# Attention stacks through DRAM: query parts written once, repeated by the reads' pattern, the rows below them read separately

## The chip, the cores and the metric

The kernel runs on one core of one Trainium2 chip. The metric is the device time of one execution in microseconds. The core has five engines with queues of their own: TensorE (PE; its weight loads are PEld), VectorE (DVE), ScalarE (ACT), GpSimd (POOL) and SyncE (SP), which issues all DMAs of this kernel. All of SP's transfers go through one queue to 16 DMA engines.

## The reference

Twelve residual sublayers on x of shape (32, 128, 128), each on the layer-normalised x: three kinds of attention, mixtures of experts, a bidirectional Mamba and a quantised network. The change is in five attentions with 16 heads of 8 dimensions. L3a is self-attention with rotated queries and keys, L1x (with a mask), L2x and L3x attend to a context of 77 rows, and L0a is causal linear attention. Cut to one of them:

```python
def _L3_xattn_ref(xq, xkv, Wq, Wkv, Wout, bout):
    scale = HEAD_DIM ** (-0.5)
    q = (xq @ Wq.T).reshape(B, SQ, NUM_HEADS, HEAD_DIM)
    kv = (xkv @ Wkv.T).reshape(B, SKV, 2, NUM_HEADS, HEAD_DIM)
    k, v = (kv[:, :, 0], kv[:, :, 1])
    att = jax.nn.softmax(jnp.einsum('bxhd,byhd->bhxy', q, k) * scale, axis=-1)
    x = jnp.einsum('bhxy,byhd->bxhd', att, v).reshape(B, SQ, H)
    return x @ Wout.T + bout
```

In L0a the scores are elu(q)+1 times elu(k)+1, masked causally, without a softmax.

## The kernel before

**Streams and order.** The 32 sequences are worked in 4 passes of two streams, 4 sequences (512 columns) each. `run_stream` (L2502) yields a due time for every step of a sublayer, and `in_turn` (L2482) merges the two streams' steps by these times. This is done once for each engine when the program is built, so each engine has one fixed order of both streams' instructions, and semaphores alone decide when they run. The second stream follows the first by 430 us of planned time (`LAG`), so its L2x meets the first stream's L0a of the next pass, and the Mamba (L2a) of either stream lies beside attentions of the other.

**Scores from parts.** A head has only 8 dimensions. `class Heads` (L792) splits each projected value into three bf16 parts (high, mid, low; `heads_high_act`, `heads_rest_dve`, `heads_mid_act`, `heads_low_dve`), and a score is the sum over all nine products of a query part with a key part. So the contraction has 3 x 3 x 8 = 72 rows (`USED`), built as a stack: row (i, j, d) of the query stack is query part i, row (i, j, d) of the key stack is key part j. Rows 72 to 127 (`ROWS` = 128) hold constants: a row of ones and zeros in the query stack, the masked keys' row (L1x) and zeros in the key stack. They were filled in DRAM at the start (`fill_first` L2829, `fill_rest` L2839) and are never written again, save the mask's row.

**Through DRAM.** The parts lie in SBUF as 128 partitions (dimension, head) x 3 parts x columns. The stack needs dimensions of one head on 72 partitions. SP does this with DMAs: `heads_write_sp` (L1351) writes the three parts to DRAM three times, once for each copy, 384 KB each for queries (L1357); `heads_read_sp` (L1361) waits for the last of them (L1365) and then reads the stack in 4 groups of 4 heads, all 128 rows, 4 KB a row, 512 KB a group (L1370). In L0a and L3a query and key parts are both written in the sublayer's main part and the 8 reads alternate: query group 0, key group 0, query group 1 and so on. In L1x, L2x and L3x the keys come from the context, and their writes and reads are issued ahead of the query's (`heads_early_sp`, L1374).

**Who uses them.** `stacks(u)` (L956) makes PE wait for a group's query and key landings at every fourth of 16 units. `scores` (L962, matmul L967) makes q k for the maxima, which DVE reduces (L1252), and `shifted` (L979, matmul L988) makes the transposed scores for the exponentials; L0a has only the latter. `scores` runs up to 6 units ahead of `shifted`.

**Mamba beside it.** `mamba_sp` (L2013) reads rows of B from DRAM onto all partitions, a pair of states at a time (L2026, 512 KB), on the same SP queue. POOL multiplies them into a state's input (L1997), DVE scans it (L2114, L2119).

The rest of the diff renames semaphores of the quantised network L3f (`qf_*` to `ff_*` and `proj_p`), so that one more is to be had.

Of the kernel before, what the change touches and what calls it, by code (L numbers as in the profile page):

```python
# [29 lines left out]
NB = 4  # L30
# [145 lines left out]
class Numbers:  # L176
# [43 lines left out]
    qf_pe="PE: quantised network", qf_a="ACT: quantised network", qf_d="DVE: quantised network",  # L220
    qf_p="Pool: quantised network",
# [5 lines left out]
    rb1="an odd pair of rows of B is on all partitions",  # L227
    wq="query parts are in DRAM", wk="key parts are in DRAM", wm="the masked keys' row is in DRAM",
# [720 lines left out]
def heads_pe(pe, g, m, A, free):  # L949
# [6 lines left out]
    def stacks(u):  # L956

        if u % 4 == 0:
            pe.wait_ge(*g.landed("rq%d" % (u // 4), A.key))
            pe.wait_ge(*g.landed("rk%d" % (u // 4), A.key))  # L960
# [477 lines left out]
def turn_pe(pe, g, m, key, src, free):  # L1438

    s = g.s  # L1440
    yield 0.04
    if key == "L3f":
        pe.wait_ge(*g.at("qf_d", "r3"))
    else:
        pe.wait_ge(*g.at("ln_xn", (key + "i" if key in NESTED else key)))
    g.wait_free(pe, free, s, 2)
    for b in range(NB):
        last = pe.transpose(m.bank[s][2][:, b * T:(b + 1) * T], src[s][:, b, :], m.const["ident"])
    last.then_inc(*g.one("ln_tr", key))
    free[s, 2] = ("ln_xT", key)  # L1450
# [781 lines left out]
def quantised_pe(pe, g, m, Q, free):  # L2232
    s = g.s
    for j in range(4):
        k = j % 2
        yield 0.06 + 0.01 * j
        pe.wait_ge(*g.at("ln_xT", "L3f"))
        g.wait_free(pe, free, s, k)
        pe.matmul(m.bank[s][k][:, :], Q.w("w1", 128 * j, 128 * j + 128), m.xT[s][:, :], start=True, stop=True)\
          .then_inc(*g.one("qf_pe", ("h", j)))  # L2240
        free[s, k] = ("qf_a", ("h", j))
    for b in range(NB + 1):
        if b < NB:
            yield Q.time(b, -0.8)
            if b == 0:
                pe.wait_ge(*g.at("qf_a", ("hs", 3)))
# [5 lines left out]
            last.then_inc(*g.one("qf_pe", ("tok", b)))  # L2252
            free[s, b % 2] = ("qf_d", ("q1", b))
        if b >= 1:
            yield Q.time(b - 1, 0.8)
            pe.wait_ge(*g.at("qf_d", ("q3", b - 1)))
# [4 lines left out]
            last.then_inc(*g.one("qf_pe", ("back", b - 1)))  # L2261
            free[s, 2] = ("qf_a", ("qT", b - 1))
    yield 0.98
    g.wait_free(pe, free, s, 3)
    pe.wait_ge(*g.at("qf_a", ("qT", NB - 1)))
# [4 lines left out]
    last.then_inc(*g.one("qf_pe", "out"))  # L2270
# [3 lines left out]
def quantised_act(act, g, m, Q):  # L2274
    s = g.s
    for j in range(4):
        yield 0.06 + 0.01 * j
        act.wait_ge(*g.at("qf_pe", ("h", j)))
        act.activation(Q.hp(s, j)[:, :, 1:T + 1], m.bank[s][j % 2][:, :].rearrange("p (b t) -> p b t", t=T),
                       ACT.Copy).then_inc(*g.one("qf_a", ("h", j)))  # L2280
    for j in range(4):
        yield 0.16 + 0.06 * j
        act.wait_ge(*g.at("qf_d", ("conv", j, 2)))
        act.activation(Q.hs(s, j), Q.hs(s, j), ACT.Silu, bias=Q.w("convb", j, j + 1))\
           .then_inc(*g.one("qf_a", ("hs", j)))
    for b in range(NB):
        yield Q.time(b, 0.85)
        act.wait_ge(*g.at("qf_pe", ("back", b)))
        act.activation(Q.qT(s)[:, :, b * T:(b + 1) * T],
                       m.bank[s][2][:, :].bitcast(BF16)[:, 0:512].rearrange("p (j t) -> p j t", t=T),  # L2290
                       ACT.Copy).then_inc(*g.one("qf_a", ("qT", b)))


def quantised_pool(pool, g, m, Q):
# [5 lines left out]
    last.then_inc(*g.one("qf_p", "pad"))  # L2300


def quantise_tokens_dve(dve, g, m, Q):
# [3 lines left out]
    def step(name, last):  # L2307
        last.then_inc(*g.one("qf_d", name))

    def after(name):  # L2310
        dve.wait_ge(*g.at("qf_d", name))
# [35 lines left out]
def quantised_dve(dve, g, m, Q):  # L2347
    s = g.s
    for j in range(4):
        for tap in range(3):  # L2350
            yield 0.12 + 0.06 * j + 0.01 * tap
            src, w = Q.hp(s, j)[:, :, tap:tap + T], Q.w("conv", 3 * j + tap, 3 * j + tap + 1)
            if tap == 0:
                dve.wait_ge(*g.at("qf_a", ("h", j)))
                dve.wait_ge(*g.at("qf_p", "pad"))
                ins = dve.tensor_scalar(Q.hs(s, j), src, w, None, ALU.mult)
            else:
                dve.wait_ge(*g.at("qf_d", ("conv", j, tap - 1)))
                ins = dve.scalar_tensor_tensor(out=Q.hs(s, j), in0=src, scalar=w, in1=Q.hs(s, j),
                                               op0=ALU.mult, op1=ALU.add)  # L2360
            ins.then_inc(*g.one("qf_d", ("conv", j, tap)))
    for b in range(NB):
        def step(name, last):
            last.then_inc(*g.one("qf_d", (name, b)))

        def after(name):
            dve.wait_ge(*g.at("qf_d", (name, b)))

        yield Q.time(b, 0.0)
        dve.wait_ge(*g.at("qf_pe", ("tok", b)))  # L2370
# [24 lines left out]
        if b >= 2:  # L2395
            dve.wait_ge(*g.at("qf_pe", ("back", b - 2)))
        step("q3", dve.tensor_scalar(Q.qb(s, b), Q.qa(s, b), ROUND, None, ALU.subtract))
    yield 0.96
    dve.reciprocal(Q.sm(s, 8), Q.sm(s, 7)).then_inc(*g.one("qf_d", "inv2"))
    dve.wait_ge(*g.at("qf_d", "inv2"))  # L2400

    dve.tensor_scalar(Q.sm(s, 8), Q.sm(s, 8), m.wsc[:, 3:4], None, ALU.mult).then_inc(*g.one("qf_d", "f"))
    yield 0.99
    dve.wait_ge(*g.at("qf_d", "f"))
    dve.wait_ge(*g.at("qf_pe", "out"))
# [493 lines left out]
```

## Time and profile before

| | |
|---|---|
| three runs, median (lowest to highest) | 4764.98 us (4752.53 to 4768.23) |
| profiled execution, its own time | 4766.72 us |
| its span, first to last instruction | 4764.2 us |
| granted TensorE clock, mean | 0.833 of full speed |
| PE, DVE busy | 3496.6 us (73%), 2955.6 us (62%) |
| ACT, POOL busy | 1970.0 us (41%), 1234.1 us (26%) |
| DMA queue of SP | 174572 packets, 323.59 MB, 20.1% of 16 engines |

Busy times are unions of the engine's instructions. The DMA share is the mean over 16 engines: 1.00 in a short window means that all 16 move data all the time, and values slightly over 1 come from packets cut at the window's edge. In a timeline each row is a run of like instructions with its start, its length and, in brackets, the idle time of the engine before it and what ended that wait. "issue" there means that the profile shows nothing that was waited for, which also happens when the record of a released instruction is missing.

### The profile page before, as it was taken

The page shows a single profiled execution, that of the slowest core. Times are in us where ns is not written, and L with a number is a line of the kernel's source. Part 1 is how long each engine was busy: PE and PEld are TensorE (multiplying, and loading weights), DVE is VectorE, ACT ScalarE, POOL GpSimd, SP SyncE. Part 2 cuts the span into 40 slices and gives each one's busy share as a digit, 9 for nine tenths or more (in the row PEclk, how much of TensorE's full clock was granted, in tenths as well). Part 3 has the DMA queues.
Part 4 walks back from the last instruction along what each step waited for, and adds up shares of the span by engine and source line. Part 5 has one row for each costly group of instructions (what it writes and reads, how often), then busy time and mean ns, then how long its engine had stood idle before and what let it go on. Part 6 is the DMA issues. An engine that isn't in the chain of part 4 may idle for free. (4 is left out here: it accounts for less than half of the span.)

```text
span 4764.2 us, 69288 instructions
## 1 busy us (share of the span) xinstructions
PE 3496.6 (73%) x25546; PEld 2337.3 (49%) x25546; DVE 2955.6 (62%) x6919; ACT 1970.0 (41%) x3470; POOL 1234.1 (26%) x1568
## 2 busy tenths in 40 slices
PE   5868867666878878665886887856589698685674
PEld 3645635334665555433575654533357465352353
DVE  4436874884554785577545488477654548738646
ACT  2423545343343444543344355434235335443333
POOL 0001451550000243253000045145100005516410
PEclk7989978777988988777898998877789799786776
DMA  7110121313121021032122112122211200211321
GB/s 237 46 47 14 39 81 42 103 55 106 66 79 62 28 76 58 29 130 73 47 100 69 39 36 81 45 88 84 104 56 52 98 10 28 80 54 45 117 101 49
DMA packets 174905, 328.00 MB, mean 69 GB/s; under 512 B 13260, under 2 KB 114988, under 8 KB 173740
## 3 DMA queue, kind: packets, MB, share of 16 engines
q1 hardware_dynamic: 174572, 323.59, 20.1%
q8 instruction: 206, 3.38, 0.3%
q14 instruction: 127, 1.04, 0.1%
HBM read 231.87 MB, written 91.67 MB: 68 GB/s over the span
## 5 line engine op out<-in xcount | busy, mean ns | idle before, releaser
L1881 PE MATMUL bank<-sb_big,sb_weights_const 128*128 128x512 f32 x512 | 376.6, 826 | 333.9 <-DVE sb_big L2119 333.2
L1434 POOL TENSOR_TENSOR sb_rs<-sb_ve,sb_weights_const 128x4 f32<-128x4 f32 x112 | 113.4, 1012 | 1757.6 <-DVE sb_ve L1420 1757.3
L1997 POOL TENSOR_TENSOR sb_big<-sb_big 128x512 f32<-128x512 f32 x384 | 496.4, 1307 | 244.9 <-DVE sb_big L2097 244.3
L1958 ACT ACTIVATE bank<-sb_big,sb_Aneg 128x512 f32<-128x512 f32 x512 | 351.7, 689 | 497.4 <-DVE sb_big L2114 392.3
L1252 DVE TENSOR_REDUCE sb_small<-bank 128x4 f32<-128x308 f32 (+1 forms) x512 | 265.9, 523 | 344.5 <-PE bank L967 340.9
L2114 DVE TENSOR_TENSOR_SCAN sb_big<-bank,sb_big 128x512 f32<-128x512 f32 x384 | 464.6, 1210 | 6.6 <-ACT bank L1958 6.3
L988 PE MATMUL bank<-sb_big 128*77 128x128 bf16 (+1 forms) x2560 | 358.1, 234 | 83.7 <-DMA sb_big<-key_parts 30.3
L988 PEld LDWEIGHTS bank<-sb_big 128*77 128x77 bf16 (+1 forms) x2560 | 274.2, 117 | 140.2 <-issue 89.8
L967 PE MATMUL bank<-sb_big 128*128 128x77 bf16 (+1 forms) x2048 | 187.4, 227 | 179.5 <-DMA sb_big<-query_parts 114.2
L1677 PEld LDWEIGHTS bank<-sb_weights_L1f,sb_big 128*128 128x128 f32 x2048 | 257.3, 191 | 109.0 <-issue 104.9
L1137 ACT ACTIVATE sb_big<-bank 77x512 f32<-77x512 f32 (+1 forms) x352 | 207.9, 593 | 228.3 <-PE bank L1009 152.4
L991 PE MATMUL bank<-sb_topT,sb_pick 128*77 128x128 bf16 (+1 forms) x2048 | 300.0, 227 | 0.0
L1881 PEld LDWEIGHTS bank<-sb_big,sb_weights_const 128*128 128x128 f32 x512 | 97.0, 236 | 407.7 <-DVE sb_big L2119 402.0
L967 PEld LDWEIGHTS bank<-sb_big 128*128 128x128 bf16 x2048 | 145.5, 112 | 304.2 <-issue 146.5
L1677 PE MATMUL bank<-sb_weights_L1f,sb_big 128*128 128x128 f32 x2048 | 275.2, 277 | 21.6 <-DVE sb_x L1746 21.6
L1746 DVE SCALAR_TENSOR_TENSOR sb_x<-bank,sb_small,sb_x 128x128 f32<-128x128 f32 x512 | 143.9, 343 | 229.8 <-PE bank L1677 226.0
L2119 DVE TENSOR_TENSOR sb_big<-bank,sb_big 128x512 f32<-128x512 f32 x384 | 263.5, 686 | 30.9 <-PE bank L1870 8.9
L1341 POOL TENSOR_TENSOR sb_topp<-sb_small,sb_weights_const 128x16 bf16<-128x16 f32 x128 | 29.5, 231 | 971.4 <-DVE sb_small L1252 971.3
L1666 PE MATMUL bank<-sb_xT,sb_weights_L1f 128*128 128x512 f32 x512 | 268.0, 610 | 3.8 <-ACT sb_big L1706 3.8
L1706 ACT ACTIVATE sb_big<-bank,sb_weights_L1f 128x512 f32<-128x512 f32 x256 | 172.3, 686 | 202.7 <-PE bank L1666 202.2
L1666 PE MATMUL bank<-sb_xT,sb_weights_L0f 128*128 128x512 f32 x512 | 242.0, 598 | 7.4 <-ACT sb_big L1700 7.4
L991 PEld LDWEIGHTS bank<-sb_topT,sb_pick 128*77 128x77 bf16 (+1 forms) x2048 | 237.0, 118 | 17.7 <-issue 13.8
(344 smaller groups left out, 8111.7 us busy)
## 6 DMA issues: line engine op xcount, KB each, us to landing
sb_big<-query_parts SPq DMA_DIRECT2D x160, 512.0 KB, 6.5
sb_big<-state_rows SPq DMA_DIRECT2D x128, 512.0 KB, 3.8
query_parts<-sb_big SPq DMA_DIRECT2D x120, 384.0 KB, 3.3
sb_big<-key_parts SPq DMA_DIRECT2D x64, 512.0 KB, 8.9
sb_big<-context_key_parts SPq DMA_DIRECT2D x64, 308.0 KB, 3.6
key_parts<-sb_big SPq DMA_DIRECT2D x48, 384.0 KB, 4.1
context_key_parts<-sb_big SPq DMA_DIRECT2D x48, 231.0 KB, 4.1
sb_big<-masked_key_parts SPq DMA_DIRECT2D x32, 308.0 KB, 3.5
```

The source lines that it names most:

```text
L967: last = pe.matmul(bank[:, n * A.Tk:(n + 1) * A.Tk], A.q(s)[0:A.rows, h, cq], A.k(s)[0:A.rows, h, ck], start=True, stop=True)
L988: last = pe.matmul(dst, A.k(s)[0:A.rows, h, ck], A.q(s)[0:A.rows, h, cq], start=True, stop=A.linear)
L991: last = pe.matmul(dst, m.pick[0:ROWS, row:row + 1].to_broadcast([ROWS, A.Tk]), m.topT[s][0:ROWS, u // 4 % 2, :], start=False, stop=True)
L1137: act.activation(A.pT(s, u).rearrange("p a b -> p (a b)"), A.psum(s, ("shifted", u))[0:A.Tk, :], ACT.Exp, scale=A.scale).then_inc(*g.one(" ...
L1252: dve.tensor_reduce(A.top(s, group)[:, 4 * b:4 * b + 4], A.psum(s, ("scores", u))[:, 0:4 * A.Tk].rearrange("p (a c) -> p a c", c=A.Tk), AX ...
L1666: pe.matmul(m.bank[s][k][:, :], X.w(name, lo, lo + 128), m.xT[s][:, :], start=True, stop=True)\
L1677: last = pe.matmul(m.bank[s][3][:, b * D:(b + 1) * D], X.h(s, e - 1, f)[:, b * T:(b + 1) * T], X.w("down" if X.gated else "w2", 128 * k, 1 ...
L1881: pe.matmul(m.bank[s][2][:, :], m.const["ident"], M.h(s, 2 * (n % 2)), start=n == 0, stop=n == NS - 1)\
L1958: act.activation(M.dA(s, half), M.dl(s, half), ACT.Exp, scale=m.Aneg[:, NS * half + n:NS * half + n + 1])\
L1997: pool.tensor_tensor(M.h(s, 2 * (n % 2) + half), M.b_rows(s, n // 2)[:, n % 2, :], M.du(s, half), ALU.mult)\
L2114: dve.tensor_tensor_scan(h, M.dA(s, half), h, 0.0, ALU.mult, ALU.add)\
L2119: dve.tensor_tensor(h, m.bank[s][1][:, :], h, ALU.mult)\
```

## The change

`heads_write_sp` writes the query parts once, to DRAM rows 0 to 23 (part, dimension). It then issues four reads of rows 72 to 127 of the stack, one for each group of heads, at once and without a wait for the write, with a landing semaphore of their own (`rp`). `heads_read_sp` reads rows 0 to 71 of the query stack with a pattern that repeats the 24 rows three times: row (j, i, d) is query part i. The key side keeps its three writes and 128-row reads, with the order of rows changed to (j, i, d) to match. `stacks` waits once more, for the last of the `rp` reads. Cut to its core:

```diff
 def stacks(u):
 
+    if u == 0:
+        pe.wait_ge(*g.landed("rp", (A.key, 3)))
     if u % 4 == 0:
         pe.wait_ge(*g.landed("rq%d" % (u // 4), A.key))
         pe.wait_ge(*g.landed("rk%d" % (u // 4), A.key))
...
     sp.wait_ge(*g.at("proj_d", (A.key, name, "low")))
-    dst = A.dram(s, name)[0:USED].rearrange("(i j d) h n -> (d h) i j n", i=3, j=3)
+    if name == "q":
+        dst = A.dram(s, name)[0:3 * DH].rearrange("(i d) h n -> (d h) i n", i=3)
+        sp.dma_start(dst, A.parts(s, name)).then_inc(*g.landing("wq", A.key))
+        for group in range(4):
+            h = slice(4 * group, 4 * group + 4)
+            sp.dma_start(A.q(s)[USED:A.rows, h, :], A.dram(s, name)[USED:A.rows, h, :])\
+              .then_inc(*g.landing("rp", (A.key, group)))
+        return
+    dst = A.dram(s, name)[0:USED].rearrange("(j i d) h n -> (d h) i j n", i=3, j=3)
     for copy in range(3):
-        sp.dma_start(dst[:, :, copy, :] if name == "q" else dst[:, copy, :, :], A.parts(s, name))\
-          .then_inc(*g.landing("w" + name, (A.key, copy)))
+        sp.dma_start(dst[:, copy, :, :], A.parts(s, name)).then_inc(*g.landing("wk", (A.key, copy)))
...
     for each in name:
-        sp.wait_ge(*g.landed("w" + each, (A.key, 2)))
+        sp.wait_ge(*g.landed("w" + each, A.key if each == "q" else (A.key, 2)))
     for group in range(4):
         h = slice(4 * group, 4 * group + 4)
         for each in name:
-            stack = A.q(s) if each == "q" else A.k(s)
-            sp.dma_start(stack[0:A.rows, h, :], A.dram(s, each)[0:A.rows, h, :])\
-              .then_inc(*g.landing(f"r{each}{group}", A.key))
+            if each == "q":
+                rows = A.dram(s, each)[0:3 * DH, h, :].rearrange("r h n -> r (h n)")
+                sp.dma_start(A.q(s)[0:USED, h, :].rearrange("p h n -> p (h n)"),
+                             rows[None, :, :].to_broadcast([3, 3 * DH, rows.shape[1]]))\
+                  .then_inc(*g.landing(f"rq{group}", A.key))
+            else:
+                sp.dma_start(A.k(s)[0:A.rows, h, :], A.dram(s, each)[0:A.rows, h, :])\
+                  .then_inc(*g.landing(f"rk{group}", A.key))
...
-        pe.wait_ge(*g.at("qf_d", "r3"))
+        pe.wait_ge(*g.at("ff_d", "r3"))
```

## Rows read from the trace of the kernel before

**Rows 1.** The page: first line; part 6 (KB each, median us to landing).

```profile
span 4764.2 us, 69288 instructions
...
sb_big<-query_parts SPq DMA_DIRECT2D x160, 512.0 KB, 6.5
query_parts<-sb_big SPq DMA_DIRECT2D x120, 384.0 KB, 3.3
```

**Rows 2.** Who waited for query_parts, then key_parts: us idle, times.

```profile
  PE bank L967: 132.0, 17
  PE bank L988: 16.7, 1
...
  PE bank L988: 30.3, 3
  PE bank L967: 9.4, 3
```

**Rows 3.** One L1x stage alone: SyncE's issues (start us, us); issue to landing.

```profile
260.55 1.61 SPq L1357 DMA_DIRECT2D query_parts<-sb_big  x3
265.41 2.01 SPq L1370 DMA_DIRECT2D sb_big<-query_parts  x4
...
DMA to landing us min/median/max: 2.6/3.3/3.9
...
DMA to landing us min/median/max: 4.0/5.3/6.5
```

**Rows 4.** The same stage by half us: last columns PEclk, DMA share, GB/s.

```profile
266.00:266.50 0.50, 0.00 (x0) 0.00 (x0) 0.00 (x0) 0.00 (x0) 0.00 (x0) 0.50 0.50 66
269.00:269.50 0.50, 0.06 (x2) 0.06 (x3) 0.00 (x0) 0.00 (x0) 0.00 (x0) 0.50 1.06 434
```

**Rows 5.** L3a beside Mamba of the other stream: SyncE and PE timeline.

```profile
861.28 1.60 SPq L1357 DMA_DIRECT2D query_parts<-sb_big  x3
864.68 1.62 SPq L1357 DMA_DIRECT2D key_parts<-sb_big  x3
869.64 0.33 SPq L1370 DMA_DIRECT2D sb_big<-query_parts  x1
...
876.04 0.59 PE L967 MATMUL bank<-sb_big 128*128 128x128 bf16 x4 [2.88 <-issue]
```

**Rows 6.** Start: a fill of 55 rows is issued; a window while it runs.

```profile
7.47 0.30 SPq L2833 DMA_DIRECT2D query_parts<-sb_big  x1
...
14.00:15.00 1.00, 0.72 (x1) 0.50 (x2) 0.00 (x0) 0.23 (x1) 0.00 (x0) 1.00 0.68 180
```

**Rows 7.** Both streams' stacks at once: SyncE, one us of it, PE.

```profile
1095.28 0.33 SPq L1370 DMA_DIRECT2D sb_big<-query_parts  x1
...
1105.00:1106.00 1.00, 0.00 (x0) 0.00 (x0) 0.00 (x0) 0.00 (x0) 0.00 (x0) 0.50 1.05 430
...
1112.48 0.44 PE L967 MATMUL bank<-sb_big 128*128 128x77 bf16 x4 [29.05 <-DMA sb_big<-query_parts]
```

**Rows 8.** First scores of other stages, PE timeline (idle before <- releaser).

```profile
619.50 0.70 PE L967 MATMUL bank<-sb_big 128*128 128x77 bf16 x8 [1.86 <-DMA sb_big<-query_parts]
...
964.36 0.44 PE L967 MATMUL bank<-sb_big 128*128 128x77 bf16 x4 [0.58 <-DMA sb_big<-query_parts]
...
1237.91 0.83 PE L967 MATMUL bank<-sb_big 128*128 128x128 bf16 x12 [3.13 <-DMA sb_big<-key_parts]
...
1388.12 1.44 PE L967 MATMUL bank<-sb_big 128*128 128x77 bf16 x16 [4.65 <-issue]
```

**Rows 9.** Mamba's rows of B beside stacks: SyncE, POOL, DVE timelines.

```profile
962.06 5.65 SPq L2026 DMA_DIRECT2D sb_big<-state_rows  x2
...
969.93 1.28 POOL L1997 TENSOR_TENSOR sb_big<-sb_big 128x512 f32<-128x512 f32 x1 [0.33 <-DMA sb_big<-state_rows]
...
974.21 1.21 DVE L2114 TENSOR_TENSOR_SCAN sb_big<-bank,sb_big 128x512 f32<-128x512 f32 x1
...
885.32 2.50 POOL L1997 TENSOR_TENSOR sb_big<-sb_big 128x512 f32<-128x512 f32 x2
```

More of the change, by code:

```diff
@@ L219 @@
     sc_in="Pool: a state's input", sc_y1="Pool: state added to the second half's y",
-    qf_pe="PE: quantised network", qf_a="ACT: quantised network", qf_d="DVE: quantised network",
-    qf_p="Pool: quantised network",
 )
@@ L227 @@
     rb1="an odd pair of rows of B is on all partitions",
+    rp="the rows below the query parts are in the stack",
     wq="query parts are in DRAM", wk="key parts are in DRAM", wm="the masked keys' row is in DRAM",
@@ L2239, in quantised_pe @@
         pe.matmul(m.bank[s][k][:, :], Q.w("w1", 128 * j, 128 * j + 128), m.xT[s][:, :], start=True, stop=True)\
-          .then_inc(*g.one("qf_pe", ("h", j)))
-        free[s, k] = ("qf_a", ("h", j))
+          .then_inc(*g.one("ff_pe", ("h", j)))
+        free[s, k] = ("ff_a", ("h", j))
     for b in range(NB + 1):
@@ L2245, in quantised_pe @@
             if b == 0:
-                pe.wait_ge(*g.at("qf_a", ("hs", 3)))
+                pe.wait_ge(*g.at("ff_a", ("hs", 3)))
             if b >= 2:
@@ L2251, in quantised_pe @@
                                     m.const["ident"])
-            last.then_inc(*g.one("qf_pe", ("tok", b)))
-            free[s, b % 2] = ("qf_d", ("q1", b))
+            last.then_inc(*g.one("ff_pe", ("tok", b)))
+            free[s, b % 2] = ("ff_d", ("q1", b))
         if b >= 1:
             yield Q.time(b - 1, 0.8)
-            pe.wait_ge(*g.at("qf_d", ("q3", b - 1)))
+            pe.wait_ge(*g.at("ff_d", ("q3", b - 1)))
             g.wait_free(pe, free, s, 2)
@@ L2260, in quantised_pe @@
                                     Q.qb(s, b - 1)[:, 128 * j:128 * j + 128], m.identb[:, :])
-            last.then_inc(*g.one("qf_pe", ("back", b - 1)))
-            free[s, 2] = ("qf_a", ("qT", b - 1))
+            last.then_inc(*g.one("ff_pe", ("back", b - 1)))
+            free[s, 2] = ("ff_a", ("qT", b - 1))
     yield 0.98
     g.wait_free(pe, free, s, 3)
-    pe.wait_ge(*g.at("qf_a", ("qT", NB - 1)))
+    pe.wait_ge(*g.at("ff_a", ("qT", NB - 1)))
     for b in range(NB):
@@ L2269, in quantised_pe @@
                              m.w2t[:, 128 * j:128 * j + 128], start=j == 0, stop=j == 3)
-    last.then_inc(*g.one("qf_pe", "out"))
+    last.then_inc(*g.one("ff_pe", "out"))
     free[s, 3] = ("x_upd", "L3f")
@@ L2299, in quantised_pool @@
             last = pool.memset(Q.hp(s, j)[:, :, at:at + 1], 0.0)
-    last.then_inc(*g.one("qf_p", "pad"))
+    last.then_inc(*g.one("proj_p", "pad"))
 def quantise_tokens_dve(dve, g, m, Q):
@@ L2307, in step @@
     def step(name, last):
-        last.then_inc(*g.one("qf_d", name))
+        last.then_inc(*g.one("ff_d", name))
     def after(name):
-        dve.wait_ge(*g.at("qf_d", name))
+        dve.wait_ge(*g.at("ff_d", name))
     yield 0.02
@@ L2395, in quantised_dve @@
         if b >= 2:
-            dve.wait_ge(*g.at("qf_pe", ("back", b - 2)))
+            dve.wait_ge(*g.at("ff_pe", ("back", b - 2)))
         step("q3", dve.tensor_scalar(Q.qb(s, b), Q.qa(s, b), ROUND, None, ALU.subtract))
     yield 0.96
-    dve.reciprocal(Q.sm(s, 8), Q.sm(s, 7)).then_inc(*g.one("qf_d", "inv2"))
-    dve.wait_ge(*g.at("qf_d", "inv2"))
-    dve.tensor_scalar(Q.sm(s, 8), Q.sm(s, 8), m.wsc[:, 3:4], None, ALU.mult).then_inc(*g.one("qf_d", "f"))
+    dve.reciprocal(Q.sm(s, 8), Q.sm(s, 7)).then_inc(*g.one("ff_d", "inv2"))
+    dve.wait_ge(*g.at("ff_d", "inv2"))
+    dve.tensor_scalar(Q.sm(s, 8), Q.sm(s, 8), m.wsc[:, 3:4], None, ALU.mult).then_inc(*g.one("ff_d", "f"))
     yield 0.99
-    dve.wait_ge(*g.at("qf_d", "f"))
-    dve.wait_ge(*g.at("qf_pe", "out"))
+    dve.wait_ge(*g.at("ff_d", "f"))
+    dve.wait_ge(*g.at("ff_pe", "out"))
     for b in range(NB):
```

26 lines of the change are left out of this document (13 added, 13 removed).

## The prediction

> **What bounds the kernel now.** No engine is full; both streams' work stands in one fixed order on each engine, so an engine that waits for one stream's transfer holds back the other stream too. I read the page first: 160 reads of query stacks and 120 writes of query parts, 40 stages (5 kinds, 4 passes, 2 streams) of 4 and 3 [rows 1]. Then who waited for them: 17 + 1 times for query stacks and 3 + 3 for key stacks, 188 us in all, PE stood idle until a stack landed [rows 2]. So 24 of 40 stages start their scores at a landing, and a change of that landing reaches the path. Then one stage step by step. With nothing beside it, L1x issues three writes at 260.55; the first lands 2.6 us later, the third at 265.4, when the reads are issued; the first read lands 4.0 us after that, 8.85 us after the first write's issue, and the others 1.28 us apart [rows 3]. By half microseconds the first read starts slowly, at 66 GB/s, and then all engines run: 434 GB/s [rows 4]. With both streams' stacks in flight it is 430 GB/s for many us [rows 7]. That is 25.6 to 27 GB/s for each of 16 DMA engines, or 0.16 us for a row's 4 KB. I use 0.16.
>
> **The write.** Two of three query writes go. In L1x, L2x and L3x (24 stages) the read can be issued at 2.6 us instead of 4.85: 2.25 us less. Four reads of the 56 rows below now follow the write on SyncE: 4 x 0.45 us of issue [rows 3], done at 2.3 us, so it issues no later. Each is 56 x 4 KB = 224 KB; if it is on 14 engines (56 = 14 x 4), 16 KB each, 0.64 us, 2.6 us for four. The write's data is through about 1.8 us after its issue, so these end at 4.4 us, or 5.7 if they too start as slowly as the reads [rows 4]. They are on the same queue ahead of the stack reads. The extra wait in front of a stage's first scores is for something that lands before these and costs nothing.
>
> **The read.** It shrinks from 128 to 72 rows, but its source is 3 copies x 24 rows, with the copy outermost. How are rows shared out? The trace has one clear case: the fill of 55 rows, while it runs alone, takes 0.68 of 16 engines and moves 180 GB/s [rows 6]: 11 engines, the largest divisor of 55 up to 16, not 16. A transfer with 3 outermost on its source and 72 on its destination would by the same pattern be on 3 engines if the source counts, on 12 if the destination alone does. No row decides that. I take 3, since the engines' shares must be equal on both sides and 3 is what divides both.
>
> The Trainium skill says this outright: DMA: Bandwidth & Descriptors, "Why a DMA increments its semaphore by 16 and not by 1", has the hardware path take the largest k up to 16 that divides the slowest dimension of both patterns, and its "Rules for kernel authors" warn that a leading zero-stride dimension of c copies confines a DMA to c engines. The 55-row row agrees with the first; nothing in this trace shows the second. By that rule the sum is the one below, without it the faster rival.
>
> On 3 engines each carries 24 rows: 24 x 0.16 = 3.84 us per group instead of 1.28. The cost, term by term:
>
> 1. First group, L1x, L2x, L3x. By the read's own fixed part (4.0 - 1.28 = 2.7 us): 2.6 + 2.7 + 3.84 = 9.1; behind the rows below it is 8.6 to 9.8. Against 8.85 that is -0.2 to +1.0; I take +0.5. Of the 24 waits [rows 2], 7 are L3a's, 4 L0a's and 3 the pass boundaries'; 10 are left here, and I count 14, since some are listed under issue, as L1x's 4.65 us [rows 8] (8 L1x, 5 L3x, where it is 0.6 us, one L2x alone): +7 us.
> 2. First group, L0a and L3a. Here reads wait for the key writes too, issued 3.4 us after the query write [rows 5], so the saved writes buy nothing: the rows below take their place, and keys end 0.2 to 1.5 us later. The first key read is queued behind the query read on the three engines, +2.56. Sum +2.8 to +4.1, taken as 3.3, in 11 stages (7 L3a, 4 L0a, the 2.88 and 3.13 us of idle among them) [rows 5, 8]: +36.
> 3. Later groups. Three engines carry 32 rows per pair of reads, 5.1 us. L3a in the second stream issues 12 matmuls of the first group at once [rows 8] and wants the second some 2.9 us after the first: +2.2, three times. The first L0a has three such steps, +6. L1x runs four units in 1.44 us [rows 8], then needs the second group: +3 in all. Together +16.
> 4. Three times (the pass boundaries) the first stream's L0a and the second's L2x read at once, and PE idles 29 us until the latter's first query stack [rows 7]. Ahead of it are 8 reads: 4 x (24 + 8) rows on each of three engines, 20.5 us instead of 10.2. Its own costs 3.84 instead of 1.28, and the shorter writes give back 1.1: +11.7 each, +35. This is the surest term.
> 5. Mamba's rows of B share the queue. In L3x one is issued 1.8 us after the stack reads and used by POOL at 969.93, 0.33 us late already; the scan of that state starts at 974.21 [rows 9], 3 us after its input is made. Four query reads and it would end about 5.0 + 15.4 + 1.3 + 0.3 = 22 us after the write's issue at 955.4, 7.5 late; less the 3 us lead, 4.5 us, three times. In L3a it would end 2.7 + 20.5 + 1.3 = 24.5 us after the reads' issue (869.9), at 894.4, against a use at 885.32 [rows 5, 9] which term 2 moves to 888.6: 5.8 late, less 1.5 of lead, 4.3, four times. Together +30. Bounds: +5 (the scans never run dry) and +50 (no lead).
>
> **Sum.** 7 + 36 + 16 + 35 + 30 = 124. Some of each stall is made up where the next wait would have been for the other stream anyway; in terms 4 and 2 all engines stand, so little. I keep 0.85: +105. Nothing is saved on PE, DVE, ACT or POOL, and the renamed semaphores cost nothing: no instruction of theirs changes. The profiled execution took 4766.72 us outside a span of 4764.2 [rows 1], 1.7 above the median 4764.98. 4766.7 + 105 = 4872. Own range: low -3 + 29 + 10 + 30 + 5 = 71, of which 0.8 stays, 4823; high 14 + 45 + 24 + 41 + 50 = 174, 4941, and 10 us for matmuls at the lower clock after longer idle (1.2 instead of 2.4 GHz, 0.50 in the windows [rows 4]), 4951. PE is at that level in such waits already, so this may be nothing.
>
> **The rivals.** (a) Faster: the destination's 72 rows set the engines, 12 of them, 6 rows each, 0.96 us a read. The first group then lands at 6.3 to 7.0 instead of 8.85, 2.2 earlier, but no stage gains more than PE waits now [rows 8]: 4 x 2.2 + 4 x 1.9 (L1x) + 4 x 0.6 (L3x) + 2.7 (last pass) = 21.5; the pass boundaries 3 x 2.5 = 8; the key writes behind the rows below cost 11 x 0.5 = 5. About -25: 4742. It decides from the point where a query read takes under about 2 us. For it: only the row count is seen to matter in the trace. Against: the source's outer count. Chance 0.11.
> (b) Three engines, but most is hidden: scans run ahead enough that term 5 vanishes and half of terms 1 to 3 is made up behind the other stream's work. 35 + 15 = 50 at most, as little as 30: 4797 to 4817. For it: in 16 stages PE does not wait for stacks at all. Against: in L3a and at the pass boundaries PE has nothing else. Chance 0.12.
> (c) No change: 12 or more engines, but the rows below delay the first read by what the writes save, or the change leaves the pattern of the reads as one plain transfer. 4757 to 4775. Chance 0.05.
> (d) Worse: three copies read the same rows at once and a packet takes 0.2 us or more, or the longer backlog on three engines blocks SyncE for the other stream's writes as well. Terms 2 to 5 by 1.4 or more: above 4955. Chance 0.04.
>
> **Numbers.** Forecast 0.68: 4872, 4823 to 4951. The range reaches down to (b): 4795 to 4955, which holds 0.8. A measurement tells 0.3% (14 us) from no change. Faster 0.11 (a), same 0.05 (c), slower 0.84 (forecast, b, d).
>
> **What would show it.** In the profile after, one L1x stage: query write to landing 2.6 us; stack reads landing 3.8 us apart, not 0.7 to 1.3; DMA share near 3/16 = 0.19 and some 77 GB/s in the windows while only they run. If the share is 0.75, I am wrong at the first step and (a) holds. In L3a the first scores start 3 us later after the query write. At the pass boundaries PE's idle time is near 41 us, not 29. POOL's waits for state rows, 0.5 us now in two, should be several us in each L3x and L3a; if they are absent, term 5 is wrong. If L1x's first stack lands before 8.6 us, the rows below are not in its way.

## The result and the profile after

| four runs each | before | after |
|---|---|---|
| median (lowest to highest) | 4764.48 us (4752.53 to 4768.23) | 4979.73 us (4971.28 to 4986.9) |
| ratio after / before | | 1.0456, 95% interval 1.0428 to 1.0483 |
| profiled execution, its own time and its span | 4766.72, 4764.2 us | 4971.28, 4969.5 us |
| mean granted TensorE clock | 0.833 | 0.819 |

The change costs 215 us, 4.6%. The forecast was +105 us with a range up to 4955: the sign was right, half of the size was missing, and the time lies outside the range.

The page of after: its first line, the engines' busy time, what the DRAM moved, and part 6, which answers to [rows 1] (KB of one, us from issue to landing; the two reads of query_parts are of different lines and have no median there).

```profile
span 4969.5 us, 69398 instructions
...
PE 3510.2 (71%) x25546; PEld 2342.7 (47%) x25546; DVE 2963.1 (60%) x6919; ACT 1970.0 (40%) x3470; POOL 1232.7 (25%) x1568
...
HBM read 231.87 MB, written 60.21 MB: 59 GB/s over the span
...
sb_big<-query_parts SPq DMA_DIRECT2D x160, 288.0 KB
sb_big<-query_parts SPq DMA_DIRECT2D x160, 224.0 KB
sb_big<-key_parts SPq DMA_DIRECT2D x64, 512.0 KB, 15.7
...
query_parts<-sb_big SPq DMA_DIRECT2D x40, 384.0 KB, 2.8
```

ACT and POOL work as long as before, DVE 7 us and PE 14 us longer. Nearly all of the loss is waiting. Far fewer bytes are written (91.67 MB before), and the time rose all the same. Who waited for query_parts, then for key_parts (us idle, times), against [rows 2]:

```profile
  PE bank L968: 224.3, 21
...
  PE bank L989: 7.6, 3
...
  PE bank L989: 68.9, 5
  PE bank L968: 63.2, 8
```

Together 364 us, before 188. PE's idle time grew by 192 us in all, and by this view 176 of them are waits for stacks. (L968 and L989 are the lines of scores and shifted now, L1358 writes the query parts, L1361 reads the rows below, L1379 reads the query stack, L1383 the key stack.)

One L1x stage with nothing beside it, as [rows 3]: SyncE and the first two groups' scores, then its microseconds (last columns PEclk, DMA share, GB/s).

```profile
271.02 0.37 SPq L1358 DMA_DIRECT2D query_parts<-sb_big  x1
271.81 1.62 SPq L1361 DMA_DIRECT2D sb_big<-query_parts  x4
274.24 2.92 SPq L1379 DMA_DIRECT2D sb_big<-query_parts  x4
282.42 0.42 PE L968 MATMUL bank<-sb_big 128*128 128x77 bf16 x4 [12.62 <-DMA sb_big<-query_parts]
...
286.15 0.44 PE L968 MATMUL bank<-sb_big 128*128 128x77 bf16 x4 [1.44 <-DMA sb_big<-query_parts]
```

```profile
275.00:276.00 1.00, 0.00 (x0) 0.00 (x0) 0.00 (x0) 0.00 (x0) 0.00 (x0) 0.50 0.93 197
276.00:277.00 1.00, 0.00 (x0) 0.00 (x0) 0.00 (x0) 0.00 (x0) 0.00 (x0) 0.50 0.88 176
...
280.00:281.00 1.00, 0.00 (x0) 0.00 (x0) 0.00 (x0) 0.00 (x0) 0.00 (x0) 0.50 0.19 78
281.00:282.00 1.00, 0.00 (x0) 0.00 (x0) 0.00 (x0) 0.00 (x0) 0.00 (x0) 0.50 0.19 78
```

There are two stretches. From 279 on only the stack reads run, at a share of 0.19 = 3/16 and 78 GB/s. That is the three engines of the forecast, and the groups' scores start 3.7 us apart (forecast 3.84). Before that, the rows below run, with the first stack read behind them on three engines, at a share near 0.9 with only 176 to 197 GB/s: nearly all engines are busy, at half the rate that a 128-row read gives them [rows 4]. They are not through until 278, seven microseconds after the write's issue, instead of 4.4 to 5.7. That is new, and the forecast lacked it.

The pass boundary, against [rows 7]: SyncE takes 12.5 us to issue the four reads of L2x's stack, where it took 2.9 us for four in the stage above, and PE stands 46.6 us instead of 29.05.

```profile
1136.24 0.74 SPq L1379 DMA_DIRECT2D sb_big<-query_parts  x1
...
1149.45 12.53 SPq L1379 DMA_DIRECT2D sb_big<-query_parts  x4
1168.45 0.41 PE L968 MATMUL bank<-sb_big 128*128 128x77 bf16 x4 [46.62 <-DMA sb_big<-query_parts]
```

The Mamba beside it: POOL's waits for rows of B (us, times, longest), and DVE's scans with the idle time in front of them; first before, then after.

```profile
POOL sb_big L1997 <- DMA sb_big<-state_rows: 0.5, 2, 0.3
...
L2114 DVE TENSOR_TENSOR_SCAN sb_big<-bank,sb_big 128x512 f32<-128x512 f32 x384 | 464.6, 1210 | 6.6 <-ACT bank L1958 6.3 <-POOL sb_big L1997 0.2
```

```profile
POOL sb_big L2010 <- DMA sb_big<-state_rows: 69.8, 11, 9.7
...
L2127 DVE TENSOR_TENSOR_SCAN sb_big<-bank,sb_big 128x512 f32<-128x512 f32 x384 | 465.0, 1211 | 46.2 <-POOL sb_big L2010 39.8 <-ACT bank L1971 6.3
```

### The profile page after: what moved, and what is told of

Same layout as the page of the kernel before. It is cut to its first block, busy times and chain, and to the rows that moved or that the text cites. A ratio compares the mean times of both kernels' runs of the same rounds, so it can differ in the third digit from the quotient of the medians.

```text
span 4969.5 us, 69398 instructions
## 1 busy us (share of the span) xinstructions
PE 3510.2 (71%) x25546; PEld 2342.7 (47%) x25546; DVE 2963.1 (60%) x6919; ACT 1970.0 (40%) x3470; POOL 1232.7 (25%) x1568
## 3 DMA queue, kind: packets, MB, share of 16 engines
q1 hardware_dynamic: 142732, 292.13, 19.3%
## 4 chain that ended last, share of the span: by engine, by line
PE 47%; DVE 21%; issue 9%; DMA 9%; ACT 7%; POOL 4%; SPq 3%; DVEq 0%; POOLq 0%; ACTq 0%
PE bank L1679 8%; PE bank L1690 7%; DVE sb_big L2127 4%; DMA sb_big<-query_parts 4%; PE bank L1010 3%; PE bank L1894 2%; PE bank L989 2%; DMA key_parts<-sb_big 2%; PE bank L546 2%; PE bank L565 2%; PE bank L491 2%; DVE sb_big L2132 2%; PE bank L935 2%; PE bank L1020 2%; PE bank L992 1%
## 5 line engine op out<-in xcount | busy, mean ns | idle before, releaser
L2127 DVE TENSOR_TENSOR_SCAN sb_big<-bank,sb_big 128x512 f32<-128x512 f32 x384 | 465.0, 1211 | 46.2 <-POOL sb_big L2010 39.8
L989 PE MATMUL bank<-sb_big 128*77 128x128 bf16 (+1 forms) x2560 | 368.2, 238 | 127.9 <-DMA sb_big<-key_parts 68.9
L968 PE MATMUL bank<-sb_big 128*128 128x77 bf16 (+1 forms) x2048 | 192.9, 231 | 316.6 <-DMA sb_big<-query_parts 180.7
L989 PEld LDWEIGHTS bank<-sb_big 128*77 128x77 bf16 (+1 forms) x2560 | 280.9, 120 | 187.7 <-issue 120.5
L968 PEld LDWEIGHTS bank<-sb_big 128*128 128x128 bf16 x2048 | 149.0, 114 | 447.9 <-issue 408.2
```

The lines of the kernel that those rows point to most:

```text
L968: last = pe.matmul(bank[:, n * A.Tk:(n + 1) * A.Tk], A.q(s)[0:A.rows, h, cq], A.k(s)[0:A.rows, h, ck], start=True, stop=True)
L989: last = pe.matmul(dst, A.k(s)[0:A.rows, h, ck], A.q(s)[0:A.rows, h, cq], start=True, stop=A.linear)
L2127: dve.tensor_tensor_scan(h, M.dA(s, half), h, 0.0, ALU.mult, ALU.add)\
```

## The experiments

**The theory after the result.** Two separate costs. First, each stack read is on three engines, as forecast. Second, the rows below cost about twice the DMA time that I gave them, because a transfer that lies within one half of the partitions gets half the rate, however many engines it is on. **Rivals:** the rows below are cheap and the three-engine reads alone cost twice the forecast, by blocking SyncE; the first reads behind a write are slow whatever they are; or the packets are slow because three copies read the same 24 rows of DRAM.

A median in this section stands beside runs of the kernel before on the same chip (4755.7 to 4756.1 us). In the section on the result before took 4764.48 us; put on the base of this section by its ratio, after is 4973 us. A difference of two kernels here is good to some 10 to 20 us, by the intervals of their ratios. "First scores" is the start of a stage's first score matmul in the trace, counted from the issue of its query write, in stages where PE waits for it; for L3a the first three passes are given.

### e6: rates of transfers by themselves

Before the first sublayer, reads of 4 KB rows from a weight array, one kind after the other and each kind waited for:

```diff
+def probes(sp, m):
...
+    for probe in (lambda: plain(0, 128), lambda: plain(72, 56), lambda: plain(0, 56), lambda: plain(64, 64),
+                  lambda: plain(32, 64), lambda: plain(0, 72), lambda: copies(True), lambda: copies(False), three):
+        made += probe()
+        sp.wait_ge(m.s_probe, 16 * made)
```

`plain(at, rows)` is four DMAs to partitions at to at + rows, `copies(True)` four with 3 copies outermost, `copies(False)` four with the 24 rows outermost and the copies inside, `three` twelve of 24 rows each.

> The kernel before, with nine probes by SyncE at the start, after the first fills, one after the other: four reads of 4 KB a row each, from an input in DRAM into the still unused tile of L1f's weights, and a wait for their landing. (1) 128 rows to partitions 0 to 127; (2) 56 rows to 72 to 127; (3) 56 rows to 0 to 55; (4) 64 rows to 64 to 127; (5) 64 rows to 32 to 95; (6) 72 rows to 0 to 71; (7) the pattern of the change, 3 copies outermost of 24 rows; (8) 24 rows outermost, each 3 times; (9) three transfers of 24 rows in the place of each one. Theory half: a transfer that lies in one half of the partitions (0 to 63 or 64 to 127) gets half the rate, however many DMA engines move it. Then (1) about 410 GB/s, (2), (3) and (4) about 200, (5) about 410, (7) 78 GB/s at a DMA share of 0.19, (8) between 150 and 310. Rival start: rows below were slow only because they followed a write, or for the first 2 us of any read. Then (2) and (3) run at 14/16 of (1), some 350 GB/s after their first 2 us, and (4) like (5). The whole run is some 60 us longer than before in its first pass alone.

One microsecond out of the middle of each kind, in the order of the list (128 rows; 56 rows at 72; 56 at 0; 64 at 64; 64 at 32; 72 at 0; copies outermost; 24 rows outermost; three transfers of 24):

```profile
25.00:26.00 1.00, 0.00 (x0) 0.00 (x0) 0.00 (x0) 0.00 (x0) 0.00 (x0) 0.50 1.02 418
...
31.00:32.00 1.00, 0.00 (x0) 0.00 (x0) 0.00 (x0) 0.00 (x0) 0.00 (x0) 0.50 0.90 188
...
38.00:39.00 1.00, 0.00 (x0) 0.00 (x0) 0.00 (x0) 0.00 (x0) 0.00 (x0) 0.50 0.93 193
...
44.00:45.00 1.00, 0.00 (x0) 0.00 (x0) 0.00 (x0) 0.00 (x0) 0.00 (x0) 0.50 1.02 197
...
52.00:53.00 1.00, 0.00 (x0) 0.00 (x0) 0.00 (x0) 0.00 (x0) 0.00 (x0) 0.50 0.84 270
...
58.00:59.00 1.00, 0.00 (x0) 0.00 (x0) 0.00 (x0) 0.00 (x0) 0.00 (x0) 0.50 0.79 180
...
75.00:76.00 1.00, 0.00 (x0) 0.00 (x0) 0.00 (x0) 0.00 (x0) 0.00 (x0) 0.50 0.19 78
...
86.00:87.00 1.00, 0.00 (x0) 0.00 (x0) 0.00 (x0) 0.00 (x0) 0.00 (x0) 0.50 0.79 229
...
93.00:94.00 1.00, 0.00 (x0) 0.00 (x0) 0.00 (x0) 0.00 (x0) 0.00 (x0) 0.50 0.73 197
```

What to see: a share near 0.9 or 1.0 can carry 418 GB/s or 190. 64 rows at partition 64 keep all 16 engines busy and move 197; the same 64 rows at partition 32, across the middle, move 270. So it isn't the number of rows or of engines alone, but where the rows lie. 56 rows (224 KB) at 188 GB/s are 1.2 us each and 4.9 us for four; I had 0.64 and 2.6. A stack read of 72 rows at 180 GB/s takes 1.6 us, longer than the 128-row read it replaces (512 KB at 418: 1.25 us). And copies outermost take the 78 GB/s that three engines give: 26 GB/s an engine, as in a full read. The rival of slow packets falls with that, and so does the rival of a slow start behind a write: the slow probes have no write in front of them, and are as slow in their middle.

Two probes do not fit the theory as I put it. I had expected 410 GB/s for the 64 rows at 32, and they got 270. The 72 rows at 0 reach over the middle with eight of them and got 180, no more than 56 rows. That transfers to one half get about half the rate is measured; what sets the rate of one that lies across the middle stays open.

The Trainium skill, SBUF — State Buffer, section "Door 1: The DMA port swizzle (why `[64,N]` ≈ `[32,N]`)", says that partitions 0 to 63 reach only 8 of the 16 SBUF ports and 64 to 127 the other 8. The probes of 56 rows at 0 and at 72 and of 64 rows at 64 agree with it (188 to 197 against 418 GB/s). By the same map 32 to 95 reach all 16, and the probe there gave 270, which is more than half but not the whole.

### e1: each group's read split into three

```diff
...
-                sp.dma_start(A.q(s)[0:USED, h, :].rearrange("p h n -> p (h n)"),
-                             rows[None, :, :].to_broadcast([3, 3 * DH, rows.shape[1]]))\
-                  .then_inc(*g.landing(f"rq{group}", A.key))
+                for copy in range(3):
+                    sp.dma_start(A.q(s)[3 * DH * copy:3 * DH * (copy + 1), h, :], A.dram(s, each)[0:3 * DH, h, :])\
+                      .then_inc(*g.landing(f"rq{group}", (A.key, copy)))
```

> The changed kernel, with each stack read of 3 x 24 rows made as three transfers of 24 rows, so that no source has 3 outermost. Theory (three engines for the read, plus half rate for the rows below): the read's terms go, the rows' stay. First stack of L1x some 8.7 to 9.5 us after the write's issue (11.3 to 12.6 after the change, 8.8 before); L3a ready at about 17.5 instead of 20.0; PE's idle time at the pass boundaries 33 us instead of 46; POOL waits for state rows under 10 us in all instead of 70. Sum 4 + 30 + 12 + few: about 4810 us. Rival issue: the time is lost in SyncE's issue of these transfers. Then twelve issues where four stood cost as much or more, and the time stays above 4930.

4835.98 us, ratio 1.0166 (1.0149 to 1.0183). Against after that is 144 us less, 138 by the ratios, for nothing but the pattern of one read. POOL's waits for rows of B fall from 69.8 to 14.1 us, DVE's scans wait 2.4 us for POOL instead of 39.8. SyncE issues the last twelve reads of the boundary in 4.87 us, where it took 12.53 for the four, so the number of issues is not what costs. But the kernel is still 80 us above before, 26 more than I expected: the rows below are left in it, and L1x's first scores come at 10.0 to 11.4 us, later than the 8.7 to 9.5 that I expected. The same boundary and the waits:

```profile
1112.86 4.87 SPq L1379 DMA_DIRECT2D sb_big<-query_parts  x12
...
1129.71 0.42 PE L968 MATMUL bank<-sb_big 128*128 128x77 bf16 x4 [36.84 <-DMA sb_big<-query_parts]
...
POOL sb_big L2009 <- DMA sb_big<-state_rows: 14.1, 7, 3.3
```

### e7, e2, e3: the rows below gone

The scores are made over 72 rows instead of 128, so that the rows below aren't needed (with them goes L1x's mask). e7 does only this, to the kernel before; e2 does it to after, and drops the four reads and the wait; e3 is e2 with e1's three reads.

```diff
-            last = pe.matmul(bank[:, n * A.Tk:(n + 1) * A.Tk], A.q(s)[0:A.rows, h, cq], A.k(s)[0:A.rows, h, ck],
+            last = pe.matmul(bank[:, n * A.Tk:(n + 1) * A.Tk], A.q(s)[0:USED, h, cq], A.k(s)[0:USED, h, ck],
...
-            sp.dma_start(A.q(s)[USED:A.rows, h, :], A.dram(s, name)[USED:A.rows, h, :])\
-              .then_inc(*g.landing("rp", (A.key, group)))
```

> The kernel before, with PE's score products over rows 0 to 71 of the stacks instead of 0 to 127 (the mask of L1x is left out); all transfers stay. A control: e2_no_rows_below and e3_three_reads_no_rows_below have this edit too, and PE was busy 105 and 77 us longer in them than in the changed kernel, at a granted clock of 0.800 and 0.813. Theory: products over fewer rows are granted a lower clock, and this alone costs 70 to 100 us here. Rival: rows cost nothing, the time is within 10 us of before, and reads of the rows below really cost only 20 to 35 us.

> The changed kernel without the four reads of the rows below; products go over 72 rows on PE, so the mask of L1x is left out. The stack reads stay as the change has them. Theory: 5.0 us of queue time in front of each first stack go, of which 2.5 were felt. First stack of L1x at 9.1 us, L3a ready at 17.3, idle at the pass boundaries 41 us, POOL's waits for state rows some 40 us instead of 70. Sum 4 + 29 + 37 + 15: about 4850 us. Rival start (the first reads after a write are slow for 2 us whatever they are): the slow start moves to the stack reads, the first stack of L1x comes at 10.5 or later, and the time stays above 4920.

> Both edits: three transfers of 24 rows for each stack read, no reads of the rows below, products over 72 rows (the mask of L1x left out). What is left of the change is the single write. Theory: first stack of L1x at 6.3 to 7.2 us after the write's issue instead of 8.85 before; 8 L1x and 5 L3x gain what PE waited, 20 us, the pass boundaries 10, L0a and L3a 5: about 4730 us, faster than before. Rival: reads of 24 rows are themselves slow (few engines or few partitions), then about as before, 4765.

e7, the control: 4813.31 us, ratio 1.0125 (1.0103 to 1.0146), +57 us, where I had expected 70 to 100. PE waits 188 us for query and key stacks, by the view of [rows 2], as in before, but it works 85 us longer and its granted clock is 0.815 instead of 0.833. Page line of e7, then of e2:

```profile
PE 3581.3 (74%) x25546; PEld 2395.4 (50%) x25546; DVE 2959.2 (62%) x6919; ACT 1971.5 (41%) x3470; POOL 1233.7 (26%) x1568
```

```profile
PE 3615.6 (73%) x25546; PEld 2417.3 (49%) x25546; DVE 2963.4 (60%) x6919; ACT 1971.9 (40%) x3470; POOL 1232.7 (25%) x1568
```

e2: 4959.45 us, ratio 1.0426 (1.0394 to 1.0458). I had expected about 4850. Read by its time alone it says that the rows below cost 20 us (14 by the ratios), which was the rival. Read with the control it says 57 more: 71 to 77. Stage by stage the first scores come nearly as my forecast described: at 9.5 to 10.1 us in L1x, L2x and L3x (forecast 9.1; after: 11.2 to 12.9), in L3a at 17.5 to 19.1 (after 19.9 to 20.7). But the whole is more than that. Against its control e7 the kernel is 146 us slower, and this is the price of the three-engine reads with the single write alone; my forecast had 105 for everything. PE's waits for stacks are 267 us against 188 in e7, and PE is busy 34 us longer, at a granted clock of 0.800 instead of 0.815.

e3: 4801.24 us, ratio 1.0105 (1.0075 to 1.0135), 12 us below the control, where I had expected 4730, faster than before. The first scores come at 6.1 to 6.5 us in the L1x that still wait. The intervals of e3 and e7 overlap, so these 12 us, all that the write-once idea is worth without its two costs, are not clear of nothing.

So the costs are seen from two sides. The rows below are 71 to 77 us where the reads are on three engines (after against e2) and 92 where they are not (e1 less e3 without its 57). The one read of three copies is 138 us with the rows below (after against e1) and 158 without (e2 against e3). Going from before by e3 and e1 to after, 4756 - 12 + 92 + 138 = 4974, must meet after's 4973, since each step is the difference of the next two kernels; it confirms nothing. What speaks for the split is that the two sides of each cost agree within 20 us. The 57 us are taken to be the same in all three kernels; PE's busy time says that they differ by some 30 between e2 and e7, so each of these terms is good to about that.

### e4: the rows apart, nothing else

Three writes as before, in the new order of rows; the stack read one plain transfer of 72 rows; the rows below as in after.

```diff
+        dst = A.dram(s, name)[0:USED].rearrange("(j i d) h n -> (d h) j i n", i=3, j=3)
+        for copy in range(3):
+            sp.dma_start(dst[:, copy, :, :], A.parts(s, name)).then_inc(*g.landing("wq", (A.key, copy)))
...
+                sp.dma_start(A.q(s)[0:USED, h, :], A.dram(s, each)[0:USED, h, :])\
+                  .then_inc(*g.landing(f"rq{group}", A.key))
```

> Only the second part of the change: queries are written three times as before, rows 0 to 71 of a stack are one plain read of 72 rows, and the rows below are four reads of their own behind the writes. Theory half: 56 rows to partitions 72 to 127 and 72 rows to partitions 0 to 71 both go at about 190 GB/s (as the probes showed), so the rows below take 5 us of the queue and a group's read 1.5 us instead of 1.28. First stack of L1x at about 11 us after the first write's issue (8.85 before), L3a ready at 19 to 20 (14.8), pass boundaries 40 us idle or more. Sum about 31 + 50 + 33: 4870 us. Rival: only the three-engine pattern is slow; then within 20 us of before.

4883.42 us, ratio 1.0255 (1.0235 to 1.0275), 13 above the expectation. Splitting 128 rows into 72 and 56 reads the same bytes over the same queue and costs 127 us, with no three-engine read anywhere and next to no wait of POOL (3.6 us). Both halves of the split are in these 127 us: the rows below, and the 72-row reads at 180 GB/s. First scores in L1x come at 12.2 to 12.9 us, in L3a at 19.3 to 19.6. Who waited for query_parts, then for key_parts, against [rows 2]:

```profile
  PE bank L968: 214.4, 19
...
  PE bank L989: 66.2, 4
  PE bank L968: 56.2, 7
```

### e5 and e8: the rows below put elsewhere

e5 puts each group's rows below in front of its three stack reads. e8 issues two or three of the four groups (those whose place in SBUF nothing else uses) before the query write, when the sublayer's input is ready.

```diff
...
+    yield A.time(-A.before + 0.1)
+    sp.wait_ge(*g.at("ln_xT", A.key))
+    for group in range(2 if A.rotated else 1, 4):
+        h = slice(4 * group, 4 * group + 4)
+        sp.dma_start(A.q(g.s)[USED:A.rows, h, :], A.dram(g.s, "q")[USED:A.rows, h, :])\
+          .then_inc(*g.landing("rp", (A.key, group)))
```

> One write; each group's rows below are read just ahead of its three transfers of 24 rows, after the write has landed, none before. Theory: 2.7 us of queue time a group (1.25 + 1.44) against 1.28 before. L1x's first stack at about 8.0 us (8.85 before), L3a at 15.1 to 15.5 (14.8), the pass boundaries some 3 us longer each. Gains of about 10 and costs of about 15: 4755 to 4775, no change that can be told. Rival: reads of the rows below are cheap wherever they stand; then some 4735.

> Three transfers of 24 rows for each stack read, and the rows below of the groups that hold no scratch (3 of 4, 2 in L3a) issued when the sublayer's xT is there, before the query parts are made; the others stay behind the write. Theory: the cost of the rows below leaves the path. L1x's first stack at 6.3 to 6.8 us after the write, L3a at 15.0 to 16.0, L0a about 14, the pass boundaries 3 to 4 us longer idle than before. Against e1_three_reads (4836) some 80 to 90 us faster: 4745 to 4760, about as before. Rival: e1's loss lies in the number of transfers SyncE issues (16 reads for 4); then it stays near 4830.

e5: 4821.5 us, ratio 1.0141 (1.0124 to 1.0158), a miss: 47 us above the upper end of what I expected. L1x was as expected but for one stage (first scores at 7.4 to 8.1, once 9.1), but where keys are read too each pair of groups is longer by 1.2 us of rows below, by the rate of e6, and L3a came at 17.3 to 19.5 us, where I had expected 15.1 to 15.5; POOL waits 33.5 us. e8: 4773.37, ratio 1.0038 (1.0024 to 1.0053), 13 us above the expected range, and still slower than before. 63 us of e1's 80 are back by moving two or three transfers of four out of the way. Two things remain in it. At the boundary PE still stands 37 us. And the first L1x of the first stream has its keys' reads and now its rows below in front of the query write:

```profile
257.31 1.77 SPq L1382 DMA_DIRECT2D sb_big<-masked_key_parts  x4
259.12 1.27 SPq L1407 DMA_DIRECT2D sb_big<-query_parts  x3
262.34 0.39 SPq L1358 DMA_DIRECT2D query_parts<-sb_big  x1
...
269.65 4.77 SPq L1379 DMA_DIRECT2D sb_big<-query_parts  x12
```

The write is issued at 262.3 behind them and takes 7.3 us to land, so that the stack reads go out 7.3 us later; in the second stream's L1x they go out after 3.1 to 3.3.

### e9 and e10: only where it could pay

e8's scheme in L1x and L3x (e9), or in L1x, L2x and L3x (e10); the other stages with the writes and the reads of before.

```diff
+WRITE_ONCE = ("L1x", "L3x")
...
+    if name == "q" and A.key not in WRITE_ONCE:
+        dst = A.dram(s, name)[0:USED].rearrange("(j i d) h n -> (d h) j i n", i=3, j=3)
+        for copy in range(3):
+            sp.dma_start(dst[:, copy, :, :], A.parts(s, name)).then_inc(*g.landing("wq", (A.key, copy)))
+        return
```

> L1x and L3x (16 stages) take e8's scheme: one query write, four groups of rows 72 to 127 of which two or three are issued before the write, three reads of 24 rows a group. L0a, L2x and L3a keep the three writes and the 128-row reads of before, with the order of rows changed to (j, i, d). Theory (the write saved is worth something only where the query's own chain sets the time, and each half-rate group of rows below costs wherever key reads or the other stream's stacks are on the queue): first stack in L1x and L3x some 6.3 us after the write's issue instead of 8.85, L3a 14.8, L0a 14.6 and PE's idle at the pass boundaries 29 us as in before. L1x saves up to 2.5 us eight times, L3x what PE waits now (0.6 us): 15 to 25 us faster than before, 4732 to 4742. Rival (the rows below disturb the other stream's reads wherever they are put): POOL's waits for state rows grow and the time is that of before or above, 4756 to 4775.

> The same with L2x too (24 stages). Theory: three of the eight L2x are the pass boundaries, where the rows below (3 x 1.1 us of work at half rate for the groups issued with the write, more for those queued with L0a's stacks) come in front of L0a's and L2x's stacks; PE's idle there goes from 29 to 30 to 33 us, three times, while the stages of the first stream gain 1 to 2 us four times: 4736 to 4748, no better than without L2x. Rival (at the boundary the two writes saved pay for the rows): some 5 us better than without L2x.

4754.09 us, ratio 0.9996 (0.9987 to 1.0005), and 4758.7 us, ratio 1.0006 (0.9996 to 1.0016): no difference from before, and a miss for both: I had expected 15 to 25 us of gain from e9 and 8 to 20 from e10. PE's idle time at the first boundary is 28.0 us in e9, about as in before (29.05), and 30.8 in e10. What became of L1x, first stream and second:

```profile
260.25 0.39 SPq L1366 DMA_DIRECT2D query_parts<-sb_big  x1
...
266.71 4.78 SPq L1387 DMA_DIRECT2D sb_big<-query_parts  x12
...
270.22 0.42 PE L968 MATMUL bank<-sb_big 128*128 128x77 bf16 x4 [11.19 <-DMA sb_big<-query_parts]
...
616.33 4.79 SPq L1387 DMA_DIRECT2D sb_big<-query_parts  x12
620.33 0.73 PE L968 MATMUL bank<-sb_big 128*128 128x77 bf16 x8
```

In the first stream the scores begin 10.0 us after the write's issue (8.9 before) and the idle time is 11.2 us instead of 10.2. In the second the wait of 1.86 us [rows 8] is gone, PE is no longer idle at this landing. Over the four passes PE's idle time there goes from 23.9 to 30.8 us in the first stream, from 7.6 to 0 in the second, and in L3x from 2.2 to 0: 3 us to win in all. The medians differ by 1.6, which is no more than noise. A stage that is ready 2.5 us earlier is worth no more here than PE waited there. I had that bound in the forecast, in rival (a), and forgot it here.

## Why the prediction was wrong

The predicted steps against what PE's idle time at landings shows, in us over the kernel before, each the sum over the stages of the term:

| step of the sum | forecast | after | e2 (no rows below) |
|---|---|---|---|
| 1. first group, L1x, L2x, L3x | 7 | 42 | 7 |
| 2. first group, L3a and L0a | 36 | 57 | 22 |
| 3. later groups | 16 | 25 | 23 |
| 4. pass boundaries | 35 | 52 | 27 |
| sum of PE's waits | 94 | 176 | 79 |
| 5. DVE's scans waiting for POOL | 30 | 40 | 41 |

**The step that failed is the price of the rows below**: 0.64 us for one, 2.6 us for four, through at 4.4 us or 5.7 after the write's issue. They are through at 7 to 7.4. That is shown three ways: by the rate alone (e6, 188 GB/s instead of 418), by making the split in the kernel before (e4, +127 us, the slower 72-row reads among them) and by taking the rows below away (71 to 92 us by e2 and e3 with their control). The table says where it went: with the rows below gone, term 1 is 7 against my 7. Its bounds, -0.2 to +1.0 a stage, contained the three engines and did not contain the half rate; +1.7 to +3.8 was measured in L1x and L3x where PE had waited before, as means of a kind of stage. The count in it, 14 stages, is one too many: four L3x wait [rows 8], not five, which is worth half a microsecond.

**It is not all that was missing.** Without the rows below the change still costs 146 us against its control (e2 against e7), and I had 105 for everything: some 40 of the missing 110 us, if not more, lie with the three-engine reads. Their engines, their rate and the waits that I priced came out, 79 us of waits and 41 of scans against 94 and 30. What I had next to nothing for is that PE itself works longer: 34 us in e2 against e7. Why more there than in after, 14 us, stays open.

**The hint was in the rows.** The fill of 55 rows moved 180 GB/s at a share of 0.68 [rows 6]. I read its share (11 engines) and used 25.6 GB/s an engine, from a read of all 128 partitions [rows 4]. The row itself says 180/11 = 16.4. At that rate 14 engines would carry 229 GB/s, which already makes the four transfers 4.0 us; the whole effect, 188, needed a probe. The fill also lay in one half: it takes `zeros(m, N)[1:]`, partitions 1 to 55. It was a bound for an unseen transfer that I drew from the farther row, though a nearer one was there.

**The three engines** were right as a mechanism: share 0.19, 78 GB/s, groups 3.7 us apart, L1x's first scores at 9.6 to 10.1 without the rows below, where I had 9.1. Rival (a) would have shown a share of 0.75 and falls. Rival (b), most of it hidden, falls as well. The Trainium skill, DMA: Bandwidth & Descriptors, section "Rules for kernel authors", warns of just this leading dimension of copies; e6's 78 GB/s and the 138 us between after and e1 agree.

**The pass boundaries**, "the surest term", 11.7 us each: 17 measured, 9 in e2. The engines' part was somewhat too large, and two sets of rows below, for which I had no term there, made up for more than that. The time lies where rival (d) had it, above 4955, to which I gave 0.04. Its packets of 0.2 us are not there: 26 GB/s an engine, as before. Its other part is: the backlog holds SyncE itself, as in the issue over 12.53 us above, and the time over which SyncE issues DMAs, summed over all, is 590 us in after, 401 in before, 505 in e1. How many of the 215 us come from that by itself is open: no run separates a held issue from the transfers that hold it.

**Mamba's rows of B** were right as a mechanism and near in size: 39.8 us of idle scans, forecast 30 (bounds 5 and 50). It belongs to the three-engine reads, not to the rows below: 41 us in e2, 2.4 in e1. What it costs in time isn't settled. PE's waits for stacks and its 14 us of longer work make 190 of the 205 us by which the span grew, so some 15 appear on PE as anything else; but a late scan can also lengthen a wait for a stack that follows it.

**The share kept, 0.85**, is not settled. In after 176 us of PE's waits and 40 of DVE's, added, are 216, and the kernel lost 215; with terms at their measured size my sum would have been 216 x 0.85 = 184, still too little. But in e1 and e4, without a three-engine read, it is near what I had or under it: e1's span grew by 70 us for 94 of such waits, e4's by 129 for 148. In e2, against e7, it is 148 us for 120. So a part of the stalls is made up there, as I said, and with three-engine reads something is added, PE's longer work among it; that the two come out nearly even in after is luck.

**The lower clock after longer idle**, for which the upper end had 10 us, is there: 0.819 instead of 0.833 over the whole, PE busy 14 us longer.

## What to carry to other kernels

Price a DMA by bytes over the rate that its own partitions get, not by its number of engines: a busy share of 1.0 can be 418 or 190 GB/s. Splitting a 128-partition transfer into 72 and 56 rows to save bytes makes both halves slow, and here the 128-row read was faster than the 72-row part of it. And before an edit that makes data ready earlier, add up what the engines wait for that data now: in e9 and e10 it brought no more than that, while what it put on the shared queue in exchange was paid in stages with nothing to gain as well. Where an experiment leaves something out, run the same omission on the kernel before: without e7, e2 reads as 20 us for the rows below instead of 71 to 77.

## What the runs showed of the hardware

- Reads of 4 KB rows from DRAM to SBUF: 418 GB/s to 128 partitions, 180 to 197 to 56, 64 or 72 of them from 0, 64 or 72 on, 270 to 64 of them from 32 on.
- A source with 24 rows outermost and 3 copies inside keeps a share of 0.79 and 229 GB/s, three times the 78 GB/s of copies outermost, for the same 72 rows, and somewhat more than the 197 of three transfers. It needs the rows of the stack in another order, and wasn't tried in the kernel.
- Scores over 72 rows of the PE array instead of 128 (e7): the same number of instructions, granted clock 0.815 instead of 0.833, PE busy 3581 instead of 3497 us, 57 us more in all. The idle times at landings are unchanged (188 us), so it is the work itself that got a lower clock. Leaving rows out of the products cost 1.2%.
- SyncE issues a read whose source has three copies outermost in 0.68 to 0.72 us, against 0.37 for each of the three 24-row reads and 0.43 for a 128-row one.
